# A first feed-forward that picks one of eight experts: from masked inputs to products of every expert, chosen by VectorE

## What is computed

```python
def _L0_ffn_ref(x, tile_sigs, W, b):
    scores = jnp.einsum('bsd,td->bst', x, jnp.sign(tile_sigs))
    idx = jnp.argmax(scores, axis=-1)
    all_out = jnp.einsum('bsd,tde->bste', x, W) + b[None, None]
    out = jnp.take_along_axis(all_out, idx[:, :, None, None], axis=2)
    return out[:, :, 0, :]
...
x = x + jnp.tanh(g_xattn[0]) * _L0_xattn_ref(_layernorm(x, axis=-1), ctx_1024, ctx_1024, ...)
x = x + jnp.tanh(g_ffn[0]) * _L0_ffn_ref(_layernorm(x, axis=-1), L0_ffn_tile_sigs, L0_ffn_W, L0_ffn_b)
x = x + jnp.tanh(g_xattn[1]) * _L1_xattn_ref(...)
...
```

## Time and profile before

| | us |
|---|---|
| median of 3 runs | 961.43 |
| lowest and highest | 956.85 and 969.81 |
| the profiled execution | 961.11 |
| its span (first to last instruction) | 959.3 |
| TensorE, VectorE, ScalarE, POOL busy | 833.1, 741.9, 506.5, 304.9 |
| the share of TensorE and of VectorE in the chain that ended last | 48%, 35% |

### The profile page before, as it was taken

How to read it: one execution, slowest core, us unless ns; L and a number is a source line. 1 busy time by engine, 2 the same in 40 slices (tenths; PEclk the granted TensorE clock), 3 DMA queues, 4 the chain that set the end, 5 groups by cost and what they waited for, 6 DMA issues and landing times.

```text
span 959.3 us, 19558 instructions
## 1 busy us (share of the span) xinstructions
PE 833.1 (87%) x7428; PEld 551.1 (57%) x7428; DVE 741.9 (77%) x1826; ACT 506.5 (53%) x799; POOL 304.9 (32%) x339
## 2 busy tenths in 40 slices
PE   3788888789889899998999888887898899999897
PEld 2443355545667688874466333474456777888543
DVE  6799998997776836778767999999977666658681
ACT  2582655356534433536895736644565444442775
POOL 5522045743443301100144020565545432111000
PEclk8999999899999899999999999999999999999999
DMA  8200000000000000000111000000000000000000
GB/s 297 98 2 2 2 1 2 1 2 3 2 1 2 1 2 1 6 2 7 30 29 45 2 3 2 1 2 1 3 3 1 1 2 1 2 1 1 1 9 18
DMA packets 13054, 14.27 MB, mean 15 GB/s; under 512 B 2916, under 2 KB 12028, under 8 KB 12708
## 3 DMA queue, kind: packets, MB, share of 16 engines
q1 hardware_dynamic: 12864, 12.88, 4.1%
q10 hardware_dynamic: 100, 0.14, 0.1%
HBM read 11.54 MB, written 1.05 MB: 13 GB/s over the span
## 4 chain that ended last, share of the span: by engine, by line
PE 48%; DVE 35%; ACT 8%; issue 6%; POOL 2%; DMA 1%; ACTq 0%; DVEq 0%
PE banks L1077 42%; DVE nm_row L1543 10%; DVE probs L1562 4%; ACT probs L1026 3%; PE banks L766 3%; DVE xn_row L1496 2%; DVE wide L1637 2%; DVE st_row L1389 2%; DVE mv_row L1391 1%; PE banks L1135 1%; ACT kT_row L951 1%; PE banks L1256 1%; DVE stack L1532 1%; DVE qr_row L1528 1%; DVE oh_row L1613 1%
## 5 line engine op out<-in xcount | busy, mean ns | idle before, releaser
L1543 DVE TENSOR_REDUCE nm_row<-banks 128x4 f32<-128x1024 f32 (+1 forms) x192 | 209.8, 1126 | 25.8 <-PE banks L1077 25.5
L867 POOL TENSOR_TENSOR rstd_row<-rstd_row,neghalf 128x2 f32<-128x2 f32 x66 | 47.8, 724 | 307.4 <-DVE rstd_row L1491 236.2
L1026 ACT ACTIVATE probs<-banks 128x1024 f32<-128x1024 f32 (+1 forms) x144 | 127.6, 930 | 25.0 <-PE banks L1077 24.8
L1077 PE MATMUL banks<-wide,c 128*128 128x256 f32 x512 | 115.7, 379 | 0.0
L1077 PE MATMUL banks<-probs,vpad 128*32 128x256 f32 (+1 forms) x1536 | 99.8, 379 | 12.2 <-ACT probs L1021 6.2
L1077 PEld LDWEIGHTS banks<-wide,c 128*128 128x128 f32 x512 | 94.9, 190 | 11.8
L1077 PE MATMUL banks<-kT_row,qT_row 48*128 48x256 bf16 (+2 forms) x896 | 88.9, 287 | 9.3 <-ACT probs L1026 4.2
L1077 PE MATMUL banks<-qT_row,kT_row 50*128 50x256 bf16 (+2 forms) x896 | 83.2, 285 | 9.0 <-ACT probs L1026 4.4
L1021 ACT ACTIVATE probs<-probs 128x1024 f32<-128x1024 f32 x64 | 67.2, 1057 | 43.6 <-DVE probs L1562 41.9
L1562 DVE TENSOR_TENSOR probs<-banks,biasT_row 128x1024 f32<-128x1024 f32 x64 | 75.6, 1216 | 6.0 <-PE banks L1077 5.6
L867 POOL TENSOR_TENSOR kss_row<-kss_row,neghalf 128x32 f32<-128x32 f32 x8 | 44.4, 5545 | 107.6 <-DVE kss_row L750 107.6
(11 more groups left out here) (227 smaller groups left out, 1555.6 us busy)
## 6 DMA issues: line engine op xcount, KB each, us to landing
c<-in_c SPq DMA_DIRECT2D x1, 2500.0 KB
wide<-in_mask SPq DMA_DIRECT2D x8, 256.0 KB, 2.8
c<-in_c SPq DMA_DIRECT2D x1, 1194.5 KB
xn_row<-in_ctx SPq DMA_DIRECT2D x8, 128.0 KB, 3.9
x_row<-in_x SPq DMA_DIRECT2D x8, 128.0 KB, 3.1
late<-in_late SPq DMA_DIRECT2D x2, 512.0 KB, 15.2
out<-x_row SPq DMA_DIRECT2D x8, 128.0 KB, 1.9
c<-in_c SPq DMA_DIRECT2D x1, 968.0 KB, 5.5
```

The costliest lines, as they stand in the source:

```text
L867: return pool.tensor_tensor(t, t, neghalf[:, 0:n], ALU.pow)
L1026: act.activation(dst[:, :, 0:w], src[:, :, 0:w], ACT.Exp, scale=1.0 if l == 2 else HD ** -0.5).then_inc(sem["probs"], 1)
L1077: return pe.matmul(dst, lhsT, rhs, start=start, stop=stop, **kw)
L1543: V.tensor_reduce(nm[b][:, t, :, 2 * jp:2 * jp + 2], ps[:, :, :, 0:kn], AX.X, ALU.max, negate=True).then_inc(sem["max"], 1)
```

## The change

In the first feed-forward the order of choosing and multiplying is turned round. TensorE multiplies the unmasked tokens with all eight experts: for each half t of 128 tokens (`every`, twice per row) xT stands still and `wf0` moves, two f32 matmuls of 512 columns into a pair of PSUM banks; the result has tokens on partitions. VectorE makes `ge` = one-hot * tanh(g) once, and adds for each expert x = product * ge[:, t, e] + x (eight `scalar_tensor_tensor` of 128x128, each linked to the one before). The bias alone goes the old way (`outer`: one matmul per half), added by the same line as before, after the last `every`. The `spread` step and the `wide` buffer fall away for this layer, and `fore` with them. The other layers' code is as before. The table of costs has 1.7 us of TensorE and 1.9 us of VectorE for one `every`. `LEAD` and `FAVOUR` have new numbers throughout, and `SAME` goes from 0.2 to 0.0, so the whole order is laid anew; the fillers go from 128 to 193.

```diff
-            out += [("spread", l, row)]
+            out += [("every", l, row, t) for t in range(NT)] if l == 0 else [("spread", l, row)]
...
-            out += [("fore", l, row)] if l == 0 else []
...
-LEAD = [[284.0, 283.1, 286.2, 284.5, 282.0, 1163.3, 210.7, -34.7],
+LEAD = [[279.5, 278.4, 279.9, 280.8, 319.5, 1679.5, 386.4, 113.0],
...
-SAME = 0.2
+SAME = 0.0
...
-        "outer": [("PE", 1.89), ("DVE", .39)], ("outer", 1): [("PE", 1.78), ("DVE", .99)],
+        "outer": [("PE", .11), ("DVE", .39)], "every": [("PE", 1.7), ("DVE", 1.9)], ("outer", 1): [("PE", 1.78), ("DVE", .99)],
...
-        "outer": [("f_ps", "one", "f_in")] if l else [],
+        "outer": [("f_ps", "one", "f_in" if l else "x_fed")], "every": [("every_ps", "two", "fed")],
...
-                    if kind in ("fore", "outer"):
+                    if kind == "every":
+                        t = s[3]
+                        pe.wait_ge(sem["xT"], at("xT", ("flip", 4, row)))
+                        claim(pe, "every_ps", s)
+                        for i in range(2):
+                            ins = mm(bank("every_ps", s)[:, i * 512:(i + 1) * 512], xT[b][:, t * P:(t + 1) * P], W("wf0")[:, i * 512:(i + 1) * 512])
+                        ins.then_inc(sem["every_ps"], 1)
+                    if kind == "outer":
                         if l == 0:
-                            t = 0 if kind == "fore" else 1
-                            if t == 0:
-                                pe.wait_ge(sem["spread1"], at("spread1", r))
-                                claim(pe, "f_ps", s)
-                            dst = bank("f_ps", s)[:, t * P:(t + 1) * P]
-                            mm(dst, ohT[b][:, t * P:(t + 1) * P], biases("bf0"), stop=False)
-                            for e in range(E):
-                                ins = mm(dst, held(wides, "wide", s)[:, e, t * P:(t + 1) * P], W("wf0")[:, e * P:(e + 1) * P], start=False, stop=(e == E - 1))
-                            if kind == "outer":
-                                ins.then_inc(sem["f_ps"], 1)
+                            pe.wait_ge(sem["onehotT"], at("onehotT", ("choose", l, row)))
+                            claim(pe, "f_ps", s)
+                            for t in range(NT):
+                                ins = mm(bank("f_ps", s)[:, t * P:(t + 1) * P], ohT[b][:, t * P:(t + 1) * P], biases("bf0"))
+                            ins.then_inc(sem["f_ps"], 1)
...
+                    if kind == "every":
+                        t = s[3]
+                        dve.wait_ge(sem["every_ps"], at("every_ps", s))
+                        dve.wait_ge(sem["x_bias"], at("x_bias", ("stats", 4, row)))
+                        if t == 0:
+                            dve.wait_ge(sem["onehot"], at("onehot", ("route", 0, row)))
+                            ch.link(V.tensor_scalar(ge[b][:, :, :], oh[b][:, :, 0, :], tg[:, 4:5], None, ALU.mult))
+                        for e in range(E):
+                            ins = V.scalar_tensor_tensor(out=x[b][:, t, :], in0=bank("every_ps", s)[:, e * P:(e + 1) * P], scalar=ge[b][:, t, e:e + 1],
+                                                         in1=x[b][:, t, :], op0=ALU.mult, op1=ALU.add)
+                            if e < E - 1:
+                                ch.link(ins)
+                        ins.then_inc(sem["fed"], 1)
...
                         if l == 0:
+                            dve.wait_ge(sem["fed"], at("fed", ("every", l, row, NT - 1)))
                             V.scalar_tensor_tensor(out=x[b][:, :, :], in0=ps, scalar=tg[:, 4:5], in1=x[b][:, :, :],
                                                    op0=ALU.mult, op1=ALU.add).then_inc(sem["x_fed"], 1)
```

More of the change, by code:

```diff
@@ L130 @@
 AHEAD = 2
-LEAD = [[284.0, 283.1, 286.2, 284.5, 282.0, 1163.3, 210.7, -34.7],
[7 rows of a table removed]
-QUIET, GAP, SHARE, FILLER, WINDOW = 0.55, 0.5, 0.5, .213, 3.4133
-SAME = 0.2
-FAVOUR = {"again": 244.4, "bias": 21.4, "choose": 33.1, "consts": -10.8, "deep": -20.8, "deep_out": -21.2, "divide": 72.0, "expand": -60.3, "fetch": 12.4,
-          "finish": -167.6, "flip": 51.8, "fold": 56.4, "fore": 178.7, "gate": 203.7, "inner": 2.2, "k_flip": 4.6, "k_low": 30.4, "k_mid": -80.9,
-          "k_turn": 18.0, "kv": 53.0, "lift": -105.5, "load": -9.6, "mask": 310.8, "max": -0.6, "mix": -1.2, "norm": 2.8, "num_flip": -3.6, "o_flip": 40.2,
-          "outer": 0.3, "plus": -52.5, "q_flip": 0.5, "q_low": 67.3, "q_mid": 39.9, "q_turn": 53.5, "query": 1.1, "route": 255.2, "shift": 55.2,
-          "shift_flip": 90.1, "split": -77.2, "spread": 6.0, "stats": 32.0, "store": 51.5, "sums_flip": 0.6, "weigh": -1.7}
+LEAD = [[279.5, 278.4, 279.9, 280.8, 319.5, 1679.5, 386.4, 113.0],
[7 rows of a table added]
+QUIET, GAP, SHARE, FILLER, WINDOW = 0.55, 0.5, 0.5, .213, 3.4133
+SAME = 0.0
+FAVOUR = {"again": 168.2, "bias": 54.7, "choose": 51.6, "consts": -23.8, "deep": -26.0, "deep_out": -38.8, "divide": 69.9, "every": -2.2, "expand": -5.8,
+          "fetch": 10.5, "finish": -167.2, "flip": 31.3, "fold": 206.9, "gate": 195.0, "inner": -23.2, "k_flip": 2.1, "k_low": 15.7, "k_mid": -39.0,
+          "k_turn": 23.4, "kv": 37.7, "lift": -133.9, "load": -41.8, "mask": 260.8, "max": -0.6, "mix": -1.2, "norm": 4.0, "num_flip": -3.3, "o_flip": 53.9,
+          "outer": -0.1, "plus": -64.7, "q_low": 93.0, "q_mid": 76.4, "q_turn": 1.1, "query": 1.4, "route": 187.1, "shift": 1.0, "shift_flip": 30.4,
+          "split": -85.3, "spread": 4.0, "stats": 10.7, "store": 144.7, "sums_flip": 0.3, "weigh": -1.8}
 COST = {"load": [("SP", .4), ("PE", .27), ("ACT", .27), ("DVE", 1.56), ("POOL", .67)], "mask": [("SP", .4)], "fetch": [("SP", .6)], "consts": [("SP", 3)],
@@ L240, in starts_after @@
         out.append((("consts", 0, ROWS - 1), "SP"))
-    if l >= 1 or kind in ("attend", "sums_flip", "num_flip", "o_flip", "route", "choose", "spread", "fore", "outer"):
+    if l >= 1 or kind in ("attend", "sums_flip", "num_flip", "o_flip", "route", "choose", "spread", "every", "outer"):
         if eng != "SP":
@@ L260, in starts_after @@
                 "spread": [(of("choose", l), "ACT")],
-                "inner": [(of("spread", l), "DVE")], "expand": [(of("spread", l), "DVE")], "fore": [(of("spread", l), "DVE")], "again": [(of("inner", l), "ACT")],
-                "outer": [(of(*[("spread", 0), ("again", 1), ("inner", 2), ("", 0)][min(l, 3)]), ["DVE", "POOL", "ACT", ""][min(l, 3)])],
+                "inner": [(of("spread", l), "DVE")], "expand": [(of("spread", l), "DVE")], "every": [(of("flip", 4), "ACT")], "again": [(of("inner", l), "ACT")],
+                "outer": [(of(*[("choose", 0), ("again", 1), ("inner", 2), ("", 0)][min(l, 3)]), ["ACT", "POOL", "ACT", ""][min(l, 3)])],
                 "deep": [(of("flip", 7), "ACT")],
@@ L297, in takes @@
             out.append(("h0_ps", "two", ("h0", l, row)))
-        if kind == "fore":
-            out.append(("f_ps", "one", ("x_fed", l, row)))
     if kind == "attend" and eng == ("DVE" if l == 0 else "ACT"):
@@ L307, in takes @@
         out.append(("mask", "wide", ("biasT_ps", 0, row)))
-    if (kind, l, eng) in (("spread", 0, "DVE"), ("spread", 2, "DVE"), ("inner", 1, "ACT")):
+    if (kind, l, eng) in (("spread", 2, "DVE"), ("inner", 1, "ACT")):
         out.append(("wide", "wide", ("f_ps", l, row)))
@@ L353, in signals @@
         own = [use for use, _, _ in psum_uses(s)]
-        if kind in ("inner", "outer") and not own:
-            own = ["h0_ps" if kind == "inner" else "f_ps"]
+        if kind == "inner" and not own:
+            own = ["h0_ps"]
         return own + {"again": ["h1_ps"], "weigh": ["weighed"]}.get(kind, [])
@@ L367, in signals @@
                 "outer": (["f_in"] if l else []) + (["y_var"] if l == 2 else ["x_fed"]),
-                "finish": ["x_fed"], "deep_out": ["x_fed"]}[kind]
+                "finish": ["x_fed"], "every": ["fed"], "deep_out": ["x_fed"]}[kind]
     if eng == "ACT":
```

2 lines of the change are left out of this document (1 added, 1 removed), and 14 rows, old and new, of the table LEAD.

## The result

The changed kernel takes 1005.18 us (median of 4 runs, 1001.09 to 1008.31), the kernel before 963.22 us beside it: a ratio of 1.044, with a 95% interval of 1.0404 to 1.0476. It is slower by some 42 us. Forecast were 981 us, with a range of 957 to 998: the direction held, the size was half, and the result lies outside the range.

A forecast was written before the change was run, and what follows sets the result against it. VectorE was taken to bound the first feed-forward's stages, TensorE the third's. VectorE's +29.7 us counted as +21.1 and TensorE's -8.1 as -1.6: +19.5 on 961.1, so 981 us, range 957 to 998.

The forecast's parts named there:

- 16 additions of VectorE per row, 7 of 8 at 0.376 us, net +3.7, +29.7 in all.: First feed-forward: linked additions and a tensor_scalar take 6.0 us per row, replacing two multiplications of 2.27 us.
- Rival 3: VectorE's additions: the link is free, starts 0.26 us apart, 16.7 us in all; +10, 971 us; chance 0.05.
- VectorE's +29.7 us counts by the share of L1637 that was on the chain, 0.71.: First feed-forward: 13.3 of 18.8 us busy time of the old one-hot products stood on the wait chain, so +21.1 us.
- 12.5 us of idle time: VectorE's idle time in the two windows, 7.2 + 5.3 us; if filled first, 17.2 of the 29.7 us remain.
- TensorE's -8.1 us counts by its share there, 0.20.: First feed-forward: TensorE saves 1.0 us per row, 8.1 in all, counted by its chain share as -1.6 us.
- The fillers: I take 0.: TensorE's 193 filler matmuls for 128 stand where VectorE is waited for: cost 0, with 10 us as the other end.
- Rival 1: First feed-forward: VectorE's slack and TensorE's relief take most of the added time; +9, 970 us; chance 0.23.
- Rival 2: TensorE and its waits for VectorE bind, additions hidden beside other rows' attention; faster, 943 us; chance 0.12.
- 10.1 us that it waited for L1637: TensorE's waits for the old one-hot products, eleven cases, part in the third feed-forward; rival 2 has them go.
- Rival 4: Additions hold PSUM banks and delay all VectorE work, 29.7 us; fillers cost up to 10; 1001 us; chance 0.15.
- The signs.: If right: additions 0.34 us, 0.37 to 0.38 apart; VectorE's sum near 772; TensorE's without fillers about 8 lower.
- VectorE above 93% in the two stages: Sign of a right forecast: VectorE that busy in the changed stage of both passes, and on most of the chain.

The follow-up runs named there:

- two sums: Changed kernel with even experts added into x, odd into another buffer, each addition waiting for the last but one, one 128x256 addition per row: 987.07 us, 1.0238.

## Why the prediction was off, step by step

- **"16 additions of VectorE per row, 7 of 8 at 0.376 us, net +3.7, +29.7 in all."** Right: 6.01 us for 16, net 3.92 with the tensor_scalar, 31.4. Rival 3, a free link, is out, though two sums show how to get most of its gain.
- **"VectorE's +29.7 us counts by the share of L1637 that was on the chain, 0.71."** This is the step that failed: measured were 1.1 to 1.4 us of kernel per us of VectorE over all sizes from 15 us up (1.6, with a wide interval, at 6.6). A line's share of the chain tells how much of that line the end followed once; that the rest had something beside it on the chain that was just as late is my reading, not shown. It is no price for more time in the same queue. As bound for the slack I had taken "12.5 us of idle time", the window less the busy sum. Some 5 us of that is what lies between one instruction and the next; the waits that a releaser ends are 4.5 and 2.7 us, and they took up nothing: in the changed kernel they were 2.7 and 5.0 us, in before with five additions per row 5.8 and 4.0. With 1.0 in place of 0.71, the measured 31.4 and nothing for TensorE the sum gives 961 + 31.4 = 992. Of the 23 us between the forecast's +19.5 and the +42 measured, this step is 10, TensorE's term below 2, and the other 11 lie over VectorE's own time, where the forecast had no term at all.
- **"TensorE's -8.1 us counts by its share there, 0.20."** The saving is real (3.60 us for the products, no spreading), but nothing of it can be seen in the time: thirty microseconds of VectorE without it lost 40, the change with it 42. (The order differs too, so this doesn't measure the term by itself.)
- **"The fillers: I take 0."** Right in the changed kernel, shown from 0 to 379; in before, 302 cost 7 us.
- **Rival 1** (slack absorbs) falls with the slope: five additions cost as much each as ten. **Rival 2** (TensorE binds) falls with the time and the chain; its "10.1 us that it waited for L1637" also added two lines of the earlier trace rows that count for the most part the same waits, 4.1 us at the matmuls and 6.0 at the weight loads. **Rival 4** forecast nearly the number, 1001, but by causes of which one does nothing (fillers). Its other half, VectorE's whole time being late, was right and had belonged in the main sum. Its sign, TensorE waiting for the banks that the additions read, was there (24.1 us), but before with ten additions lost as much per us of VectorE (1.3) with none of those waits. So its number was near for a reason that is only half its own.
- **The signs.** Additions of 0.35 us, 0.376 apart, and VectorE's sum came as said. VectorE above 93% in the two stages did not: it was 91 and 90%. TensorE's sum without fillers can't be set beside before's, for it rose with the lower clock: the changed kernel without any filler has 839 us.
- **The remaining 2 to 11 us over VectorE's own time.** In before with ten additions the stretch from the last final addition of the first feed-forward to that of the second is longer than in before by 5.7 us in the first pass and 5.3 in the second (132.2 and 127.2 against 126.5 and 121.9), and TensorE's mean clock in it is 0.87 and 0.92 against 0.95 and 0.99. With twenty in the first row alone, at 0.92 and 0.99, it is longer by 1.1 and 0; with twenty in the last, at 0.91 and 0.94, by 2.8 and 2.0. This fits the scene above, if the lower clock reaches more often into work that TensorE binds when TensorE has starved longer. It is a likely cause and not shown: twice the fillers held that clock at 0.99 in the first pass of the changed kernel and shortened the stretch by only 1.9 us (135.6 to 133.7), fillers themselves taking slots. It stays open.

## What to carry to other kernels

Before giving an engine more work, list the waits in its queue, each with its releaser. Work put directly ahead of such a wait cost next to nothing up to its length here (11 us, in one pass of one stage), where the releaser, TensorE, was full and kept its own time. Elsewhere it cost 1.1 to 1.4 per us at 90% busy and 0.8 at 63%: the waits further behind took up little or nothing. (That their releasers came later as well is the likely reason, not shown.) Window less busy sum is no slack, and a line's share of the chain is no price. Where additions must follow each other, run two sums in turn, so that none waits for the one right in front of it.

## What the runs showed of the chip that I had not expected

- Linked scalar_tensor_tensor of 128x128 out of PSUM start 0.376 us apart when each waits for the one in front, and 0.26 when each waits for the last but one.
- The granted clock of a stage that VectorE binds fell from 0.87 to 0.71 for 1.8 us in 79, and from 0.88 to 0.67 for 3.7 in 75 (no fillers), and one fall of some 12 us to the lower level (1.2 GHz) cost some 5 us where TensorE was full (a mix 0.5 us late at 310 us, 5.3 us late at 342). What a fall costs depends on where it comes, within some ten microseconds.
